# Loads in two parts and scatters of full height in the routing stage of a graph layer with experts

## The chip, the core and the metric

The kernel runs on one core of a Trainium2 chip. The time is device time in microseconds, from the first to the last instruction; the number compared is the median of several executions. The engines are PE (TensorE), DVE (VectorE), ACT (ScalarE), POOL (GpSimd) and SP (SyncE, which here only starts DMAs); sixteen DMA engines move the data.

## What is computed

6250 nodes of 256 features go through a graph attention layer with 8 heads and 200000 edges, then through a layer of 8 experts, of which each node uses the best two. Cut to what matters (`_layernorm`, `elu` and `top_k` are the usual ones):

```python
def gnn(x, src, trg):                     # x normed
    proj = (x @ Wp.T).reshape(-1, H, FO)
    s = leaky_relu(sum(proj * a_src)[src] + sum(proj * a_trg)[trg], 0.2)
    exp_s = exp(s - max(s))
    attn = exp_s / (segment_sum(exp_s, trg)[trg] + 1e-16)
    out = segment_sum(proj[src] * attn[:, :, None], trg)
    return elu(out + x @ Wskip.T + bias)
def ffn(x):                               # x normed
    top_p, top_idx = top_k(softmax(x @ Wr + br), 2)
    weights = top_p / top_p.sum()
    y = gelu((_layernorm(x) * ln_g + ln_b) @ W1 + b1) @ W2 + b2      # for each expert
    return sum(weights * y[top_idx])
x = x + gnn(_layernorm(x), src, trg)
x = x + ffn(_layernorm(x))
```

## The kernel before

It is one program of six stages, and each ends at a barrier of all engines: `edge_tables`, `node_phase` (projections, and the rows of the skip connection, which go to DRAM as `skip_rows`), `edge_phase` (gathers, softmax and sums per node; the longest), `route_phase`, `expert_phase` and `combine_phase`. Nodes are kept 125 to a tile (`NP`), 50 tiles (`NT`), since 50 x 125 is 6250; a node is a partition.

The change touches `route_phase`. It works in 10 chunks of 5 tiles (`C = 5`, `CHUNKS`), one after another, with two buffers of what is loaded and sent. For each chunk:

- SP loads the skip rows (`r_skin`, L923) and x (`r_xin`, L926), each as one DMA of 125 partitions x 5 rows of 1 KB, 640 KB. From the third chunk on it waits until VectorE has used the buffer (`skin_used`, `x_used`).
- VectorE divides the sums by the softmax denominator (L955), adds the skip rows (L960), takes the positive part plus x (L963), while ScalarE computes 1 - exp, floored at 0, for the negative part (`ex`, L1107 and L1109); L968 joins the two. Then come mean and variance, the first norm (`xl`, L989, read by PE for the logits), the choice of the two best experts (L1003 to L1021), each node's place among those of its expert (L1027 to L1035, from counts by PE), and the second norm (`r_xn`, L1042), which is what the experts get. ScalarE copies that for the second expert (L1125).
- GpSimd sends each node's row of 257 words (256 features and the row that its result goes to) into `tokens_by_expert` (in the code `xg`), an indirect DMA for each tile and each of its two experts: ten scatters of 125 rows a chunk (L1183), to the rows in `slot`.

```python
nc.gpsimd.indirect_dma_start(
    xg, bass.IndirectOffsetOnAxis(ap=slot[b][:, 2 * u + k:2 * u + k + 1], axis=0),
    xn[b][:, u, k, :], None).then_inc(sent[b], 16)
```

The order on each engine is the order written here. VectorE runs one chunk ahead with the first part: `attention(c + 1)`, `choose(c)`, `residual(c + 1)`, `places(c)`, `first_deviation(c + 1)`, `second_norm(c)`, `first_norm(c + 1)`. At the stage's end VectorE turns the counts into whole numbers (`count_ready`), on which SP starts eight DMAs of 256 rows that write `padding` behind each expert's tokens (L932) and waits for them; GpSimd waits for its last scatters.

The last stage, `combine_phase`, already loads and stores in the two parts of `NODE_PARTS`, 112 and 13 partitions (L1481).

Of the kernel before, what the change touches and what calls it, by code (L numbers as in the profile page):

```python
# [12 lines left out]
F32 = mybir.dt.float32  # L13
F32R = mybir.dt.float32r
BF16 = mybir.dt.bfloat16
I32 = mybir.dt.int32
# [68 lines left out]
def gnn_ffn(nc, x, src, dst, Wp, a_src, a_trg, Wskip, bias, Wr, br, ln_g, ln_b, W1, b1, W2, b2, out):  # L85
    table = nc.dram_tensor("proj_table", (N, ROW), F32).ap()
    skip_rows = nc.dram_tensor("skip_rows", (N, D), F32).ap()
    xg = nc.dram_tensor("tokens_by_expert", (NX * CAP, XROW), F32).ap()

    y2 = nc.dram_tensor("results_by_token", (2 * N + P, D), F32).ap()  # L90

    with ExitStack() as ctx:
        def sb(name, shape, dt=F32):
            return ctx.enter_context(nc.sbuf_tensor(name, shape, dt))

        banks = ctx.enter_context(nc.psum_tensor("banks", [P, 8, 512], F32))
        bank = [banks[:, k, :] for k in range(8)]
        m = dict(
            banks=banks,
            iota=sb("iota", [P, P]), iota_p=sb("iota_p", [P, 1]), ident=sb("ident", [P, P]),  # L100
            lower=sb("lower", [P, P]), ones=sb("ones", [P, P]), zero16=sb("zero16", [P, ROW], BF16),
            begun=ctx.enter_context(nc.semaphore("begun")),
            cap_row=sb("cap_row", [P, NX]), ident_r=sb("ident_r", [P, P], F32R),
            acc=sb("acc", [NP, NT + 2, ROW]), neg_bound=sb("neg_bound", [P, 1]),
            ln_eps=sb("ln_eps", [P, 1]), eps=sb("eps", [P, 1]),
            gaps=sb("gaps", [NP, NT]), warm=[sb(f"warm{k}", [P, 1]) for k in range(3)], weights=sb("weights", [NP, NT, 2]),
            result_row=sb("result_row", [NP, NT, 2]), counts=sb("counts", [1, NX, 4], I32),
            br=sb("br", [NP, NX]), wr=sb("wr", [P, KD, NX]),
        )
        with ExitStack() as edge_ctx:  # L110
            def esb(name, shape, dt=F32):
                return edge_ctx.enter_context(nc.sbuf_tensor(name, shape, dt))

            m.update(src_tab=esb("src_tab", [P, COLS], I32), dst_tab=esb("dst_tab", [P, COLS]),
                     place_tab=esb("place_tab", [P, (STEPS + AHEAD) * G]), key_tab=esb("key_tab", [P, (STEPS + AHEAD) * G]),
                     inside_tab=esb("inside_tab", [P, (STEPS + AHEAD) * G]),
                     base_tab=esb("base_tab", [P, STEPS + AHEAD]), tile_int=esb("tile_int", [1, 1 + STEPS + AHEAD], I32),
                     upper=esb("upper", [P, 1 + STEPS + AHEAD]), nextt=esb("nextt", [P, 1 + STEPS + AHEAD]),
                     passes=esb("passes", [1, 1], I32), st_parts=esb("st_parts", [P, NT + 2, ZC], BF16))
            edge_tables(nc, m, bank, src, dst)  # L120
            node_phase(nc, m, bank, x, Wp, a_src, a_trg, Wskip, bias, Wr, br, table, skip_rows)
            edge_phase(nc, m, bank, table)
        route_phase(nc, m, bank, x, skip_rows, xg)
        expert_phase(nc, m, bank, xg, y2, ln_g, ln_b, W1, b1, W2, b2)
        combine_phase(nc, m, y2, out)
# [742 lines left out]
def route_phase(nc, m, bank, x, skip_rows, xg):  # L868


    with ExitStack() as ctx:
        def sb(name, shape, dt=F32):
            return ctx.enter_context(nc.sbuf_tensor(name, shape, dt))
# [6 lines left out]

        C = 5
        CHUNKS = NT // C
        xin, skin = ([sb(f"{s}{b}", [NP, C, D]) for b in range(2)] for s in ("r_xin", "r_skin"))
        den = sb("den", [NP, NT, H])
        att, positive, ex = sb("att", [NP, C, D]), sb("positive", [NP, C, D]), sb("ex", [NP, C, D])
        stats, mv = sb("r_stats", [NP, C, 6]), sb("r_mv", [NP, NT, 2])
        std1, rstd1, var2, std2, rstd12 = (sb(s, [NP, NT]) for s in ("std1", "rstd1", "var2", "std2", "rstd12"))
        xl, xlt = sb("xl", [NP, C, D]), sb("xlt", [P, C * KD, NP])
        xn = [sb(f"r_xn{b}", [NP, C, 2, XROW]) for b in range(2)]
        logits, top8, pick8 = sb("logits", [NP, C, NX]), sb("top8", [NP, C, 8]), sb("pick8", [NP, C, 8], U32)  # L890
        pick, one = sb("pick", [NP, C, 2]), sb("one", [NP, C, 2, NX])
        mask = [sb(f"mask{b}", [NP, 1 + C, NX], BF16) for b in range(2)]
        lower16, ones16 = sb("lower16", [NP, NP], BF16), sb("ones16", [NP, NP], BF16)
        place, junk = sb("place", [NP, C, 2]), sb("junk", [NP, C, 2, NX])
        slot = [sb(f"slot{b}", [NP, C * 2], I32) for b in range(2)]
        padding = sb("padding", [P, FILL // P, XROW])
        crow, cwhole = sb("count_row", [1, 6, NX]), sb("count_whole", [1, NX], I32)
        wtmp = sb("wtmp", [NP, NT])
# [7 lines left out]
        xl_ready, xlt_psum, xlt_ready, logit_psum, mask_ready, ranked, slot_ready, xn_first, xn_ready = (sem(s) for s in (  # L906
            "xl_ready", "xlt_psum", "xlt_ready", "logit_psum", "mask_ready", "ranked", "slot_ready", "xn_first", "r_xn_ready"))
        dve_step, end_step, weight_exp = sem("route_step"), sem("end_step"), sem("weight_exp")
        counted, count_ready, filled = sem("counted"), sem("count_ready"), sem("filled")
        block = ctx.enter_context(nc.Block())  # L910

        def of(c):
# [2 lines left out]
        @block.sync  # L915
        def _(sp):
            def chunk(rows, c):
                return rows[c * C * NP:(c + 1) * C * NP, :].rearrange("(u p) d -> p u d", u=C)

            for c in range(CHUNKS):  # L920
                if c >= 2:
                    sp.wait_ge(skin_used, c - 1)
                sp.dma_start(skin[c % 2][:], chunk(skip_rows, c)).then_inc(skin_loaded[c % 2], 16)  # L923
                if c >= 2:
                    sp.wait_ge(x_used, c - 1)
                sp.dma_start(xin[c % 2][:], chunk(x, c)).then_inc(xin_loaded[c % 2], 16)  # L926
            sp.wait_ge(count_ready, 1)

            with sp.Fori(0, NX) as e:
                n = nc.values_load(m["counts"][0:1, bass.ds(e, 1), 0:1].rearrange("p a k -> p (a k)"),  # L930
                                   engines=[sp.engine], min_val=0, max_val=N)
                sp.dma_start(xg[bass.ds(e * CAP + n, FILL), :].rearrange("(h p) d -> p h d", p=P), padding[:]  # L932
                             ).then_inc(filled, 16)
            sp.wait_ge(filled, 16 * NX)

        @block.vector
        def _(dve):
# [12 lines left out]
            def attention(c):  # L950
                b = c % 2
                x1 = m["acc"][:, of(c), 0:D].rearrange("p u (h f) -> p u h f", h=H)
                if c:
                    dve.wait_ge(ex_ready, c)
                step(nc.vector.tensor_tensor(  # L955
                    att[:].rearrange("p u (h f) -> p u h f", h=H), x1,
                    den[:, of(c), :].unsqueeze(3).to_broadcast([NP, C, H, FO]), ALU.mult))
                settle()
                dve.wait_ge(skin_loaded[b], 16 * (c // 2 + 1))
                nc.vector.tensor_tensor(att[:], att[:], skin[b][:], ALU.add).then_inc(skin_used, 1)  # L960
                dve.wait_ge(skin_used, c + 1)
                dve.wait_ge(xin_loaded[b], 16 * (c // 2 + 1))
                nc.vector.scalar_tensor_tensor(positive[:], att[:], 0.0, xin[b][:], ALU.max, ALU.add).then_inc(x_used, 1)  # L963

            def residual(c):
# [58 lines left out]
            def places(c):  # L1024
                b = c % 2
                dve.wait_ge(ranked, c + 1)
                step(nc.vector.tensor_tensor(junk[:], one[:], rank_bank.unsqueeze(2).to_broadcast([NP, C, 2, NX]), ALU.mult))  # L1027
                with nc.allow_low_precision("whole numbers up to 50"):
                    step(nc.vector.tensor_reduce(mask[1 - b][:, 0, :], mask[b][:].rearrange("p v e -> p e v"), X, ALU.add))
                dve.wait_ge(dve_step, steps[0] - 1)  # L1030
                step(nc.vector.tensor_reduce(place[:], junk[:], X, ALU.add))
                settle()
                if c >= 2:
                    dve.wait_ge(sent[b], 16 * 2 * C * (c // 2))
                nc.vector.scalar_tensor_tensor(slot[b][:].rearrange("p (u k) -> p u k", k=2), pick[:], float(CAP), place[:],  # L1035
                                               ALU.mult, ALU.add).then_inc(slot_ready, 1)
                nc.vector.tensor_copy(xn[b][:, :, :, D], m["result_row"][:, of(c), :]).then_inc(slot_ready, 1)

            def second_norm(c):
                for u in range(C):  # L1040
                    t = c * C + u
                    nc.vector.tensor_scalar(xn[c % 2][:, u, 0, 0:D], x1_of(t), mv[:, t, 0:1], rstd12[:, t:t + 1],  # L1042
                                            ALU.subtract, ALU.mult).then_inc(xn_first, 1)

            step(nc.vector.tensor_scalar(den[:], m["acc"][:, 0:NT, D:ROW], m["eps"][0:NP, :], None, ALU.add))
# [58 lines left out]
        def _(act):  # L1104
# [17 lines left out]

            def second_copy(c):
                act.wait_ge(xn_first, C * (c + 1))
                nc.scalar.copy(xn[c % 2][:, :, 1, 0:D], xn[c % 2][:, :, 0, 0:D]).then_inc(xn_ready, 1)  # L1125

            exponential(0)
            deviations(0)
# [45 lines left out]

        @block.gpsimd
        def _(pool):
            for c in range(CHUNKS):
                b = c % 2
                pool.wait_ge(slot_ready, 2 * (c + 1))
# [354 lines left out]
```

## Time and profile before

| | us |
|---|---|
| median of 3 executions | 3241.75 (3241.1 to 3244.08) |
| span of the profiled execution | 3796.4 |
| routing stage in the profiled execution | 2835.7 to 3050.7 |

The profiled execution is a run of its own, with the profiler on, and its own time is that span: 554.65 us, 17%, longer than the median. Positions and durations below are of that execution, in microseconds from its start. A row of the timeline shows when an instruction began, how long it ran, and in brackets how long its engine had stood idle before it and what ended the wait. A row of the windows shows, for a stretch of time, how long each engine was busy, the mean busy share of the sixteen DMA engines, and what they moved.

### The profile page before, as it was taken

To read this page: it belongs to the slowest core of one execution; us is meant where nothing else is said; L and a number is where in the kernel's file an instruction comes from. 1 tells how busy PE (TensorE), PEld (TensorE's weight loads), DVE (VectorE), ACT (ScalarE), POOL (GpSimd) and SP (SyncE) were. 2 spreads that over 40 slices of the span, in tenths; PEclk is the share of its full clock that TensorE was granted. 3 is DMA by queue.
4 is the path that set the end of the run, shared out by engine and by line. 5 is a ranking of instruction groups with operands and counts; after the bars stand their busy time and mean duration, and the time that the engine had idled before them with its cause. 6 is when DMAs were issued, how large, how long until landed. Compare 5 with 4: busy or idle time off the path is not lost. (4 is left out here: it accounts for less than half of the span.)

```text
span 3796.4 us, 46157 instructions
## 1 busy us (share of the span) xinstructions
PE 2122.9 (56%) x12432; PEld 1788.7 (47%) x12433; DVE 1956.5 (52%) x5386; ACT 890.4 (23%) x2271; POOL 1821.9 (48%) x2025
## 2 busy tenths in 40 slices
PE   3755454544545554545455455444543359999990
PEld 3434343433434443434334334333433359999990
DVE  6545444444444444444444444444458746666654
ACT  1221111111111111111111111111114435555540
POOL 1026655656556656656565565655635722222110
PEclk7976767677777667677677776776765579999995
DMA  1333322323233333323333333322324442222116
GB/s 54 113 96 84 86 80 81 85 78 85 80 81 83 86 83 85 84 81 83 81 84 81 81 83 83 85 80 80 85 63 144 117 118 65 68 90 67 44 44 207
DMA packets 163652, 326.51 MB, mean 86 GB/s; under 512 B 41487, under 2 KB 95742, under 8 KB 163628
## 3 DMA queue, kind: packets, MB, share of 16 engines
q0 software_dynamic: 98560, 256.53, 24.7%
q1 hardware_dynamic: 45528, 50.33, 4.4%
q10 hardware_dynamic: 19540, 19.40, 1.6%
q8 instruction: 7, 0.11, 0.0%
q14 instruction: 17, 0.14, 0.0%
HBM read 278.03 MB, written 47.99 MB: 86 GB/s over the span
## 5 line engine op out<-in xcount | busy, mean ns | idle before, releaser
L626 POOL DMA_INDIRECT rows<-proj_table,idx x1568 | 1492.1, 952 | 1028.6 <-DVE weighed L741 612.9
L670 PE MATMUL banks<-weighed,onehot 128*128 128x264 f32 x3136 | 1147.8, 528 | 1293.5 <-DVE weighed L741 1232.4
L670 PEld LDWEIGHTS banks<-weighed,onehot 128*128 128x128 f32 x3136 | 783.1, 263 | 1475.0 <-issue 1312.5
L725 DVE TENSOR_REDUCE target<-banks 128x32 f32<-128x96 f32 x393 | 100.6, 256 | 1193.0 <-remote 1108.5
L741 DVE TENSOR_TENSOR weighed<-rows,banks 128x1024 f32<-128x1024 f32 x392 | 474.5, 1211 | 0.0
L845 ACT ACTIVATE banks<-score,neg_bound 128x32 f32<-128x32 f32 x392 | 114.1, 291 | 1387.8 <-DVE score L734 1069.5
L840 ACT CAST onehot_t<-banks 128x512 bf16<-128x512 f32 x395 | 228.2, 578 | 764.3 <-remote 740.0
L1441 POOL DMA_INDIRECT results_by_token<-yrow,goes_to x104 | 109.1, 1049 | 478.2 <-DVE yrow L1389 350.7
L707 DVE TENSOR_TENSOR onehot<-banks,key_tab 128x512 f32<-128x512 f32 x397 | 270.9, 683 | 0.0
L1328 ACT ACTIVATE hid<-banks,params 128x256 f32<-128x256 f32 x416 | 197.9, 477 | 267.5 <-PE banks L1284 261.1
L1284 PE MATMUL banks<-f_xth,w1h 128*128 128x256 f32 x832 | 236.4, 284 | 27.2 <-ACT hid L1328 14.9
L1377 DVE TENSOR_TENSOR hidl<-hid,hidh 128x256 fp32r<-128x256 f32 x416 | 169.9, 424 | 149.6 <-ACT hidh L1322 138.0
L1284 PE MATMUL banks<-f_xtl,w1h 128*128 128x256 f32 x832 | 234.4, 282 | 0.0
L1284 PE MATMUL banks<-f_xth,w1l 128*128 128x256 f32 x832 | 234.3, 282 | 0.0
L649 PEld LDWEIGHTS banks<-ident,onehot 128*128 128x128 bf16 x1584 | 150.6, 117 | 102.6 <-issue 48.2
L649 PE MATMUL banks<-ident,onehot 128*128 128x128 bf16 x1584 | 184.7, 250 | 3.8 <-DVE onehot L707 2.7
L1183 POOL DMA_INDIRECT tokens_by_expert<-r_xn,slot x100 | 130.5, 1305 | 103.8 <-issue 96.4
L1284 PEld LDWEIGHTS banks<-f_xth,w1h 128*128 128x128 f32 x832 | 158.4, 190 | 31.1 <-ACT hid L1328 16.4
L1297 PE MATMUL banks<-w2h,hidh 128*128 128x256 f32 x832 | 170.5, 286 | 0.0
L1297 PE MATMUL banks<-w2l,hidh 128*128 128x256 f32 x832 | 166.1, 281 | 0.0
L1297 PE MATMUL banks<-w2h,hidl 128*128 128x256 f32 x832 | 165.9, 281 | 0.0
L1322 ACT CAST hidh<-hid 128x256 fp32r<-128x256 f32 x416 | 161.2, 401 | 0.0
(236 smaller groups left out, 2901.1 us busy)
## 6 DMA issues: line engine op xcount, KB each, us to landing
rows<-proj_table,idx POOLq DMA_INDIRECT x1568
w_raw<-in_L_ffn_W_dram POOLq DMA_DIRECT2D x16, 1024.0 KB
xrow<-tokens_by_expert SPq DMA_DIRECT2D x106, 128.5 KB
c_y<-results_by_token SPq DMA_DIRECT2D x10, 1120.0 KB
proj_table<-trow ACTq DMA_DIRECT2D x50, 128.9 KB
xin<-in_x_dram SPq DMA_DIRECT2D x50, 125.0 KB
skip_rows<-srow ACTq DMA_DIRECT2D x50, 125.0 KB
r_skin<-skip_rows SPq DMA_DIRECT2D x10, 625.0 KB
```

Of the source, the lines that this page charges most:

```text
L626: nc.gpsimd.indirect_dma_start(rows[k][:, i, :], None, table, bass.IndirectOffsetOnAxis(ap=idx[pair][:, col:col + 1], axis=0)).then_inc(ga ...
L649: mm = nc.tensor.matmul(turn_bank[s % 2][:, i * P:(i + 1) * P], onehot16[s % ROUND][:, i, :], ident16[:], start=True, stop=True)
L670: mm = nc.tensor.matmul(acc_bank[u // 2 % 2][:, 0:ROW], onehot[u][:, i, :], weighed[:, k * SET + i, :], start=(u % 2 == 0 and i == 0), sto ...
L707: nc.vector.tensor_tensor(onehot[s % ROUND][:], node_row[s % 2].unsqueeze(1).to_broadcast(shape), m["key_tab"][:, bass.ds(ROUND * SET * it ...
L741: nc.vector.tensor_tensor(weighed[:, k * SET:(k + 1) * SET, 0:D].rearrange("p s (h f) -> p s h f", h=H), rows[k][:, :, 0:D].rearrange("p s ...
L840: nc.scalar.copy(onehot_t[s % BUF][:], turn_bank[s % 2][:]).then_inc(turn_copied[s % BUF], 1)
L1183: nc.gpsimd.indirect_dma_start(xg, bass.IndirectOffsetOnAxis(ap=slot[b][:, 2 * u + k:2 * u + k + 1], axis=0), xn[b][:, u, k, :], None).the ...
L1284: mm = nc.tensor.matmul(h_bank[j % HB][:, 0:TOK], w[:, s, k, at], v[:, k, :], start=(k == 0 and n == 0), stop=(k == KD - 1 and n == 2))
L1297: mm = nc.tensor.matmul(y_bank[h][:, 0:D], v[:, j, h * P:(h + 1) * P], w[:, s, j, :], start=(j == 0 and n == 0), stop=(j == JH - 1 and n = ...
L1322: nc.scalar.copy(hidh[:, j, :], hid[:, j, :]).then_inc(hid_high, 1)
L1328: nc.scalar.activation(hid[:, j, :], h_bank[j % HB][:, 0:TOK], ACT.Gelu, bias=params[:, s, B1 + j:B1 + j + 1]).then_inc(h_ready[j % HB], 1)
L1377: nc.vector.tensor_tensor(hidl[:, j, :], hid[:, j, :], hidh[:, j, :].bitcast(F32), ALU.subtract).then_inc(hid_low, 1)
```

## The change

Each of the twenty loads becomes two, of partitions 0 to 111 and 112 to 124, and VectorE waits for both. `r_xn` and `slot` get 128 partitions. GpSimd fills them at the start of the stage: `slot` with numbers of spare rows behind the experts' rows (of which `tokens_by_expert` gets 128 more), `r_xn` from partition 96 on with zeros; VectorE later writes the first 125 partitions of both as before. The scatters then send all 128 partitions. VectorE waits for the filling (`cleared`) ahead of its first L963.

```diff
-    xg = nc.dram_tensor("tokens_by_expert", (NX * CAP, XROW), F32).ap()
+    xg = nc.dram_tensor("tokens_by_expert", (NX * CAP + P, XROW), F32).ap()
...
+        SPARE = NP // 32 * 32
...
-        xn = [sb(f"r_xn{b}", [NP, C, 2, XROW]) for b in range(2)]
+        xn = [sb(f"r_xn{b}", [P, C, 2, XROW]) for b in range(2)]
...
-        slot = [sb(f"slot{b}", [NP, C * 2], I32) for b in range(2)]
+        slot = [sb(f"slot{b}", [P, C * 2], I32) for b in range(2)]
...
-                sp.dma_start(skin[c % 2][:], chunk(skip_rows, c)).then_inc(skin_loaded[c % 2], 16)
+                for part in NODE_PARTS:
+                    sp.dma_start(skin[c % 2][part], chunk(skip_rows, c)[part]).then_inc(skin_loaded[c % 2], 16)
...
-                sp.dma_start(xin[c % 2][:], chunk(x, c)).then_inc(xin_loaded[c % 2], 16)
+                for part in NODE_PARTS:
+                    sp.dma_start(xin[c % 2][part], chunk(x, c)[part]).then_inc(xin_loaded[c % 2], 16)
...
-                dve.wait_ge(skin_loaded[b], 16 * (c // 2 + 1))
+                dve.wait_ge(skin_loaded[b], 16 * len(NODE_PARTS) * (c // 2 + 1))
...
+                if c == 0:
+                    dve.wait_ge(cleared, 4)
...
-                dve.wait_ge(xin_loaded[b], 16 * (c // 2 + 1))
+                dve.wait_ge(xin_loaded[b], 16 * len(NODE_PARTS) * (c // 2 + 1))
...
         @block.gpsimd
         def _(pool):
+            for b in range(2):
+                nc.gpsimd.iota(slot[b][:], [[1, 2 * C]], base=NX * CAP + (2 * b - NP * 4) * C,
+                               channel_multiplier=4 * C).then_inc(cleared, 1)
+                pool.wait_ge(cleared, 2 * b + 1)
+                nc.gpsimd.memset(xn[b][SPARE:P], 0.0).then_inc(cleared, 1)
+                pool.wait_ge(cleared, 2 * b + 2)
```

The other lines of the diff write `[0:NP]` where VectorE and ScalarE write `slot` and `r_xn`.

SP's queue at the start of the routing stage, before (a row is an instruction; the names are tile and tensor, and what it waits for stands in brackets):

```order
L915 UNCONDITIONAL_BRANCH [waits barrier_Pool_Activation_PE_DVE_SP_release]
L923 DMA r_skin<-skip_rows 125x5x256
L926 DMA r_xin<-in_x_dram 125x5x256
L923 DMA r_skin<-skip_rows 125x5x256
L926 DMA r_xin<-in_x_dram 125x5x256
L923 DMA r_skin<-skip_rows 125x5x256 [waits skin_used]
```

and of the change:

```order
L916 UNCONDITIONAL_BRANCH [waits barrier_Pool_Activation_PE_DVE_SP_release]
L925 DMA r_skin<-skip_rows 112x5x256
L925 DMA r_skin<-skip_rows 13x5x256
L929 DMA r_xin<-in_x_dram 112x5x256
L929 DMA r_xin<-in_x_dram 13x5x256
L925 DMA r_skin<-skip_rows 112x5x256
L925 DMA r_skin<-skip_rows 13x5x256
L929 DMA r_xin<-in_x_dram 112x5x256
L929 DMA r_xin<-in_x_dram 13x5x256
L925 DMA r_skin<-skip_rows 112x5x256 [waits skin_used]
```

Eight DMAs in place of four lie ahead of the first wait, and the x of the first chunk stands third and fourth. GpSimd's queue at the same place, of the change (before, the branch was followed at once by the first scatter):

```order
L1180 UNCONDITIONAL_BRANCH [waits barrier_Pool_Activation_PE_DVE_SP_gather]
L1183 IOTA slot 128x10
L1186 MEMSET r_xn 32x2570 [waits cleared]
L1183 IOTA slot 128x10 [waits cleared]
L1186 MEMSET r_xn 32x2570 [waits cleared]
L1194 DMA tokens_by_expert<-r_xn,slot 53376x257 [waits r_xn_ready,slot_ready,cleared]
```

Four instructions stand ahead of the scatters, each behind the one before it. VectorE's order is the same; of the change, from the stage's start (L963 of before is L968 here):

```order
L1050 TENSOR_SCALAR den<-acc,eps 125x400
L1052 RECIPROCAL den<-den 125x400 [waits route_step]
L958 TENSOR_TENSOR att<-acc,den 125x1280 [waits route_step]
L963 TENSOR_TENSOR att<-att,r_skin 125x1280 [waits skin_loaded0,route_step]
L968 SCALAR_TENSOR_TENSOR positive<-att,r_xin 125x1280 [waits xin_loaded0,skin_used,cleared]
```

The last of these rows has one more thing to wait for, `cleared`.

## Rows read from the trace of the kernel before

**Rows 1.** The page, first line.

```profile
span 3796.4 us, 46157 instructions
```

**Rows 2.** Timeline, start of the routing stage; columns: start us, us, engine, line, operation [idle before].

```profile
2835.75 0.28 SPq L923 DMA_DIRECT2D r_skin<-skip_rows  x1
...
2835.79 0.43 DVE L1045 TENSOR_SCALAR den<-acc,eps 125x400 f32<-125x400 f32 x1 [0.32 <-PEq L549]
2836.46 1.77 SPq L926 DMA_DIRECT2D r_xin<-in_x_dram  x1
...
2838.94 1.49 DVE L955 TENSOR_TENSOR att<-acc,den 125x1280 f32<-125x1280 f32 x1
...
2844.66 1.49 DVE L960 TENSOR_TENSOR att<-att,r_skin 125x1280 f32<-125x1280 f32 x1 [4.23 <-DMA r_skin<-skip_rows]
...
2847.49 1.36 ACT L1109 ACTIVATE ex<-ex,ones 125x1280 f32<-125x1280 f32 x1
...
2850.40 1.49 DVE L963 SCALAR_TENSOR_TENSOR positive<-att,r_xin 125x1280 f32<-125x1280 f32 x1 [4.25 <-DMA r_xin<-in_x_dram]
...
2852.70 1.48 DVE L968 TENSOR_TENSOR acc<-positive,ex 125x1280 f32<-125x1280 f32 x1
```

**Rows 3.** Windows: stretch, us, busy of PE, PEld, DVE, ACT, POOL, PEclk, DMA share, GB/s.

```profile
2840.00:2850.00 10.00, 0.00 (x0) 0.00 (x0) 1.92 (x2) 3.76 (x3) 0.00 (x0) 0.50 0.34 110
...
3043.00:3047.00 4.00, 0.00 (x0) 0.00 (x0) 0.00 (x0) 0.00 (x0) 0.08 (x1) 0.50 0.83 211
...
3057.00:3059.00 2.00, 0.00 (x0) 0.00 (x0) 0.00 (x0) 0.00 (x0) 0.00 (x0) 0.50 1.06 359
3728.00:3732.00 4.00, 0.00 (x0) 0.00 (x0) 2.48 (x7) 0.00 (x0) 0.00 (x0) 0.50 1.01 257
```

**Rows 4.** Timeline, middle of the routing stage, VectorE and GpSimd.

```profile
2865.86 0.20 DVE L1003 TENSOR_TENSOR logits<-banks,br 125x40 f32<-125x40 f32 x1 [1.99 <-PE banks L1152]
...
2874.16 1.70 DVE L989 TENSOR_SCALAR xl<-acc,r_mv,rstd 125x256 f32<-125x256 f32 x5
...
2882.66 0.20 DVE L1003 TENSOR_TENSOR logits<-banks,br 125x40 f32<-125x40 f32 x1 [1.93 <-PE banks L1152]
...
2899.84 0.20 DVE L1003 TENSOR_TENSOR logits<-banks,br 125x40 f32<-125x40 f32 x1 [1.74 <-PE banks L1152]
...
2908.31 1.89 DVE L989 TENSOR_SCALAR xl<-acc,r_mv,rstd 125x256 f32<-125x256 f32 x5
...
2910.59 2.49 POOL L1183 DMA_INDIRECT tokens_by_expert<-r_xn,slot  x1 [1.77 <-ACT r_xn L1125]
```

**Rows 5.** By line: duration ns min/median/max, first and last start; the last row is L1441's.

```profile
L1183 POOL DMA_INDIRECT tokens_by_expert<-r_xn,slot x100: 1175/1187/2493, 2876.6 to 3041.9; - x100
L626 POOL DMA_INDIRECT rows<-proj_table,idx x1568: 943/949/1146, 247.8 to 2807.8; - x196
L1441 POOL DMA_INDIRECT results_by_token<-yrow,goes_to x104: 972/993/1382, 3096.7 to 3713.7; - x104
DMA to landing us min/median/max: 2.4/2.4/3.9
```

**Rows 6.** Waits in the routing stage, GpSimd: us in total, times, longest.

```profile
POOL tokens_by_expert L1183 <- ACT r_xn L1125: 7.4, 5, 1.8
```

**Rows 7.** Timeline, end of the routing stage, GpSimd and SP.

```profile
3029.85 15.26 SPq L932 DMA_DIRECT2D tokens_by_expert<-padding  x8
...
3041.90 1.18 POOL L1183 DMA_INDIRECT tokens_by_expert<-r_xn,slot  x1 [0.30 <-issue]
```

**Rows 8.** Waits of SP's queue in the routing stage: us in total, times, longest.

```profile
SPq L923 <- DVE att L960: 73.1, 7, 14.9
...
SPq L871 <- DMA tokens_by_expert<-padding: 4.5, 1, 4.5
```

**Rows 9.** Timeline, start of the program: a long GpSimd memset and VectorE beside it.

```profile
1.95 11.53 POOL L180 MEMSET acc<- 125x13728 f32 x1
...
2.35 11.21 DVE L213 TENSOR_SCALAR ident<-iota,iota_p 128x128 f32<-128x128 f32 x1
```

More of the change, by code:

```diff
@@ L908, in route_phase @@
         dve_step, end_step, weight_exp = sem("route_step"), sem("end_step"), sem("weight_exp")
-        counted, count_ready, filled = sem("counted"), sem("count_ready"), sem("filled")
+        counted, count_ready, filled, cleared = sem("counted"), sem("count_ready"), sem("filled"), sem("cleared")
         block = ctx.enter_context(nc.Block())
@@ L1034, in places @@
                     dve.wait_ge(sent[b], 16 * 2 * C * (c // 2))
-                nc.vector.scalar_tensor_tensor(slot[b][:].rearrange("p (u k) -> p u k", k=2), pick[:], float(CAP), place[:],
+                nc.vector.scalar_tensor_tensor(slot[b][0:NP].rearrange("p (u k) -> p u k", k=2), pick[:], float(CAP), place[:],
                                                ALU.mult, ALU.add).then_inc(slot_ready, 1)
-                nc.vector.tensor_copy(xn[b][:, :, :, D], m["result_row"][:, of(c), :]).then_inc(slot_ready, 1)
+                nc.vector.tensor_copy(xn[b][0:NP, :, :, D], m["result_row"][:, of(c), :]).then_inc(slot_ready, 1)
             def second_norm(c):
@@ L1041, in second_norm @@
                     t = c * C + u
-                    nc.vector.tensor_scalar(xn[c % 2][:, u, 0, 0:D], x1_of(t), mv[:, t, 0:1], rstd12[:, t:t + 1],
+                    nc.vector.tensor_scalar(xn[c % 2][0:NP, u, 0, 0:D], x1_of(t), mv[:, t, 0:1], rstd12[:, t:t + 1],
                                             ALU.subtract, ALU.mult).then_inc(xn_first, 1)
@@ L1124, in second_copy @@
                 act.wait_ge(xn_first, C * (c + 1))
-                nc.scalar.copy(xn[c % 2][:, :, 1, 0:D], xn[c % 2][:, :, 0, 0:D]).then_inc(xn_ready, 1)
+                nc.scalar.copy(xn[c % 2][0:NP, :, 1, 0:D], xn[c % 2][0:NP, :, 0, 0:D]).then_inc(xn_ready, 1)
             exponential(0)
```

## The prediction

> **What bounds the kernel now.** I began with the page: a span of 3796.4 us under the profiler [rows 1]. The median of the runs without it is 3241.75 us, 555 us less, and no view says where these 555 us lie. So the terms below are absolute microseconds of the routing stage (2835.7 to 3050.7 of the span, some 6% of it), and I subtract them from the median; if everything there shrank by 3241.75/3796.4 the sum would shrink by a seventh, which I keep for the range. The chain that ended last names only the combine stage's loads, so the rest is read from the timeline.
>
> *Start of the stage* [rows 2]. SP issues the first skip load at 2835.75 and the first x load at 2836.46. VectorE has its own work done at 2840.43 (den, reciprocal, first product) and then stands idle twice: 4.23 us until the skip rows are in, 4.25 us until x is in. Nothing else runs. The loads move at 110 GB/s with the 16 DMA engines busy 0.34 on average [rows 3], which is what five busy engines of sixteen would show (0.31). One load is 640 KB, 5.7 us at that rate. The first wait ends 8.9 us after the first issue, so 3.2 us of it are fixed (start and completion).
>
> *Middle.* From chunk to chunk VectorE's step L1003 comes at 2865.86, 2882.66, 2899.84: periods of 16.80 and 17.18 us [rows 4]. No load is waited for any more. VectorE is the pace; it waits 1.7 to 2.0 us a chunk for the logits, on a chain that runs through its own norms. GpSimd is nearly as long: ten scatters of 1.19 + 0.30 us, two of them stretched by about 1 us each (one took 2.49), are some 17 us; it waits for ScalarE's copy only five times, 7.4 us in all [rows 4 to 6].
>
> *End.* The last scatter is issued at 3041.90 and takes 1.18. SP issues the eight padding DMAs from 3029.85 to 3045.11 [rows 7] and then waits 4.5 us for them, until 3049.6 [rows 8]. A scatter lands 2.4 us after its issue in the expert stage [rows 5], so GpSimd would be through at about 3045.5. The padding ends this stage, and SP's pitch (15.26 us for eight) sets most of it.
>
> **Part 1: loads of 112 and 13 partitions.** The same bytes in two DMAs. If 112 partitions use 16 engines at the same rate for each engine as now, the rate is 110/5 × 16 = 352 GB/s: 1.8 us for a 640 KB pair. Two rows bound it: the expert weights, loaded in rows of 1 KB on all engines, run at 359 GB/s; the combine stage, whose loads have this very 112/13 split, begins at 257 GB/s with the engines all busy (1.01) [rows 3], which gives 2.5 us.
> The Trainium skill says the same of the engines (DMA: Bandwidth & Descriptors, "Why a DMA increments its semaphore by 16 and not by 1"): a DMA uses the largest number up to 16 that divides its outermost sizes, 5 for 125, 16 for 112, 13 for 13. By that rule, the share of 0.34 agrees.
> Working: at 352 GB/s the skip rows are in at 2835.75 + 3.2 + 1.8 = 2840.75, x at 2842.55. Then L960 starts at 2840.75. ScalarE's ex is ready 4.19 us after L960 starts (in the rows L960 at 2844.66, L1109 over at 2848.85), so at 2844.95; L968 starts 2.30 us after L963 (2850.40 to 2852.70), so at 2844.85. The later one counts: 2845.0 instead of 2852.70, a gain of **7.7 us**. At 257 GB/s: skip 2841.5, x 2844.0, L968 at 2846.3, gain **6.4**. I take **7.4**, nearer the first, since it is these same tensors whose rate per engine is known. VectorE's wait of 8.5 us doesn't go whole: what is late next is ScalarE's ex.
> SP's extra issues cost nothing: the unblocked ones are some 0.7 us apart, four are 2.8 us, and x's second half is issued at about 2837.9, 3.2 us before 2841.1, earlier than its data anyway. In the middle SP waits 73.1 us on VectorE [rows 8], so twenty more issues hide there.
>
> **Part 2: iota and memset on GpSimd, and VectorE's wait for them before L963.** The memset is 2570 elements per partition. The one row of a large GpSimd memset is 13728 elements in 11.53 us [rows 9], 0.84 ns each, so 2.2 us, twice, plus two iotas of about 0.15 us and three handovers of some 0.2: done about 5.3 us after 2835.7, at 2841.0. L963 is due at 2842.5. The cover is 1.5 us, so no cost; without cover (memsets at twice the time) it would be 3 us. Queued behind the wait on VectorE are L963 and everything after it. But rows 9 also show a VectorE TENSOR_SCALAR that took 11.21 us beside that memset, and L1045 is such an operation. Here the iota and a semaphore lie ahead of the memset, L1045 goes at 2835.79 and lasts 0.43. I charge **0.2 us** (behind the iota); the other end is one memset, 2.2 us, of which 0.3 is covered by the skip rows: 1.9.
>
> **Part 3: scatters of 128 rows.** For GpSimd's time the rows give two answers. By rows: 1.187 × 128/125 = 1.22 us. By form: the 128-row scatter of the expert stage takes 0.993 (median), the 128-row gather 0.949 [rows 5], against 1.187 for 125 rows, though it has 3 rows more. I take 0.99: same direction, nearly the same row length. GpSimd then needs some 2 us less per chunk. Since VectorE is the pace, little of it counts. What does count is that L989 takes 1.70 us before the scatters begin and 1.89 beside them [rows 4], and that the period was 16.80 once and then 17.18. The full difference over nine chunks would be 3.4 us; I take a third where GpSimd now has idle time just before the next copy is ready, **1.0 us**. With 1.22 us a scatter, GpSimd would need 0.3 more a chunk against a slack of about 0.17: 1.2 us lost. Range -1.2 to 3.4.
> At the end ten shorter scatters finish 2 us or more earlier, but the padding bounds there. The engines are busy 0.83 at 211 GB/s from 3043 to 3047, after the last scatter's issue [rows 3]: padding is queued behind scatters. Alone, a 256-row DMA should land about 2.9 us after its issue (2.4 of the 128-row scatter, and 0.5 for the other half at that rate): 3048.0 in place of 3049.6. Range 0 to 1.6, taken **1.0**. The spare rows add 3 × 1028 B each, 0.3 MB in all, 1 us spread over the stage, hidden.
>
> **Sum:** 7.4 - 0.2 + 1.0 + 1.0 = 9.2 us, 3241.75 - 9.2 = **3232.6 us**. All bounds on the good side give 7.7 + 3.4 + 1.6 = 12.7 (3229.0); on the bad side 6.4 - 1.9 - 1.2 + 0 = 3.3 (3238.5). The stages after it start earlier and are otherwise the same.
>
> **Rivals.**
> *A, the memset holds VectorE.* L1045 waits out a memset, as in rows 9, or the clearing ends after L963 is due. The gain falls by 1.9 to 3: 9.2 - 1.9 = 7.3, 3234.4; at worst 3235.6. For it: the 11.21 us. Against: the iota and the handover come first.
> The Trainium skill has this as a rule (SBUF — State Buffer, "Who interferes with whom"): a VectorE operation in a two-port mode, which TENSOR_SCALAR can be, and a GpSimd instruction exclude each other, and the one that issues first keeps the port for its whole length. By that rule the order of starts decides; rows 9 agree.
> *B, the loads are no faster.* 1 KB rows may be limited by something other than the number of engines, or the stage's fixed latencies grow with four DMAs; then only the 2 us of part 3 stay: 3239.8. Against: 359 GB/s at the same row length.
> *C, slower: GpSimd becomes the pace.* Its ten scatters are within 0.2 us of VectorE's period. If one takes x us more, nine chunks lose 9 × (10x - 0.17). Against the 7.2 us of the start that breaks even at x = 0.1; at x = 0.3 (1.49 us a scatter) it is 25 us, 3241.75 - 7.2 + 25.5 = 3260. For it: descriptors for all engines instead of some could cost GpSimd more. Against: both 128-row forms are shorter than the 125-row form.
> *D, the split is made but the stall isn't on the unprofiled path as long,* everything a seventh smaller: 8 us, 3233.9.
>
> **Chances.** Forecast, with D in it, 0.68; A 0.12; B 0.12; C 0.05; 0.03 for what I don't see. A measurement of this kernel tells 0.2% (6.5 us) from no change. Faster by over that: 0.65 of the forecast, 0.08 of A, 0.02: 0.75. Within: 0.03 + 0.04 of A + 0.12 of B: 0.19. Slower: C and 0.01: 0.06. The range 3228 to 3239 holds the forecast's bounds and A; it leaves out B and C.
>
> **What would show it.** In the trace of the changed kernel: VectorE's idle time before L960 and L963 under 1 us each in place of 4.2; DMA share near 1 in the first 4 us of data; L968 of chunk 0 some 9.5 us after L1045, not 16.9; L1045 at 0.43 us (several us means A); two memsets of about 2.2 us; scatters of about 0.99 us and a wait for ScalarE's copy in every chunk (none, and a period above 17.2, means C); SP's wait for the padding near 3 us in place of 4.5. Wrong outright: a stall of the same length at the start, or a loss in a later stage.

## The result: 6 us faster, with a loss at the stage's end that the sum did not hold

| | kernel before | changed kernel |
|---|---|---|
| median of 20 runs each, us | 3243.31 | 3237.18 |
| range of the runs, us | 3241.10 to 3248.68 | 3234.75 to 3240.23 |
| span of the trace, us | 3238.8 | 3235.1 |

The ratio is 0.9981, with a 95% interval of 0.9974 to 0.9987: 6.1 us less, where 9.2 were forecast. The time lies in the forecast range (3228 to 3239). It is 0.4 us short of the 0.2% (6.5 us) that the prediction set as the least that can be told from no change: by its own bins the outcome is "within", which it gave 0.19, and not the faster one with 0.75. The interval lies wholly on the faster side of 1.

The kernel before was traced again, beside the experiments (run e1_base below); its span there was 3238.8 us, near its time, and not 3796.4 as in [rows 1]. The routing stage was as long in both traces, 213.9 and 214.8 us. The 555 us lay ahead of the stage (`den` came at 2835.79 in the first trace, and at 2278.11 in the second), the stage's microseconds were true ones, and nothing had to be scaled down. "Before" is this second trace from here on.

The stage begins with VectorE's `den` (L1045, now L1050) and ends when all engines have passed the barrier that closes it (L871; the first instruction behind it is ScalarE's table load, 0.1 us later). Other lines moved as well: L960, L963, L968 are now L963, L968, L973; L1003 is L1008; L1183 is L1194.

**The start.** Timeline of the changed kernel: start, us, engine, line, operation, with the idle time before it in brackets.

```profile
2282.75 1.10 SPq L925 DMA_DIRECT2D r_skin<-skip_rows  x2
2282.79 0.43 DVE L1050 TENSOR_SCALAR den<-acc,eps 125x400 f32<-125x400 f32 x1 [0.32 <-PEq L549]
2282.98 2.42 POOL L1186 MEMSET r_xn<- 32x2570 f32 x1
2283.91 0.85 SPq L929 DMA_DIRECT2D r_xin<-in_x_dram  x2
...
2285.67 2.24 POOL L1186 MEMSET r_xn<- 32x2570 f32 x1
...
2288.49 1.49 DVE L963 TENSOR_TENSOR att<-att,r_skin 125x1280 f32<-125x1280 f32 x1 [1.05 <-DMA r_skin<-skip_rows]
...
2291.42 1.49 DVE L968 SCALAR_TENSOR_TENSOR positive<-att,r_xin 125x1280 f32<-125x1280 f32 x1 [1.45 <-DMA r_xin<-in_x_dram]
...
2293.73 1.48 DVE L973 TENSOR_TENSOR acc<-positive,ex 125x1280 f32<-125x1280 f32 x1
```

The same place of the kernel before, second trace:

```profile
2278.11 0.43 DVE L1045 TENSOR_SCALAR den<-acc,eps 125x400 f32<-125x400 f32 x1 [0.32 <-PEq L549]
...
2286.59 1.49 DVE L960 TENSOR_TENSOR att<-att,r_skin 125x1280 f32<-125x1280 f32 x1 [3.85 <-DMA r_skin<-skip_rows]
...
2292.33 1.49 DVE L963 SCALAR_TENSOR_TENSOR positive<-att,r_xin 125x1280 f32<-125x1280 f32 x1 [4.25 <-DMA r_xin<-in_x_dram]
...
2294.62 1.48 DVE L968 TENSOR_TENSOR acc<-positive,ex 125x1280 f32<-125x1280 f32 x1
```

The two waits of [rows 2] are now 1.05 and 1.45 us. The residual (L973, once L968: it joins the two parts) starts 10.94 us after `den` in place of 16.51: 5.6 us gained. Against the first trace, where it was 16.91, it would be 6.0. `den` waited 0.32 us in both kernels, so the clearing held it up by nothing, and the clearing is over at 2287.91, 3.5 us before L968 wants it.

Windows of the changed kernel: stretch, us, busy time of PE, PEld, DVE, ACT, POOL, then PEclk, DMA share, GB/s.

```profile
2285.00:2286.00 1.00, 0.00 (x0) 0.00 (x0) 0.97 (x2) 0.00 (x0) 0.87 (x3) 0.50 1.10 353
2286.00:2289.00 3.00, 0.00 (x0) 0.00 (x0) 1.95 (x2) 0.00 (x0) 1.90 (x1) 0.50 1.13 243
2289.00:2293.00 4.00, 0.00 (x0) 0.00 (x0) 2.50 (x3) 2.94 (x3) 0.00 (x0) 0.50 1.13 227
```

All sixteen engines are busy, against a third of them in [rows 3]. But the rate is 353 GB/s for one microsecond only, and then 243 and 227, below both of the prediction's rates (352 and 257).

**The middle.** The logits step of chunks 1 and 2, the changed kernel:

```profile
2323.68 0.20 DVE L1008 TENSOR_TENSOR logits<-banks,br 125x40 f32<-125x40 f32 x1 [1.93 <-PE banks L1157]
...
2340.47 0.20 DVE L1008 TENSOR_TENSOR logits<-banks,br 125x40 f32<-125x40 f32 x1 [1.93 <-PE banks L1157]
```

The period, from one chunk's logits step to the next, is 16.8 us here and in all later chunks. In the second trace of before the first period was 16.80 too, as in [rows 4], and the eight later ones 17.15 to 17.22. The groups by line and shape (busy us, mean ns), with the scatters (ns min/median/max) and GpSimd's wait for ScalarE's copy (us, times, longest), say where it comes from. The changed kernel:

```profile
L994 DVE TENSOR_SCALAR xl<-acc,r_mv,rstd 125x256 f32<-125x256 f32 x50 | 17.0, 406 | 0.0
L1047 DVE TENSOR_SCALAR r_xn<-acc,r_mv,rstd 125x256 f32<-125x256 f32 x50 | 17.0, 407 | 0.0
...
L1194 POOL DMA_INDIRECT tokens_by_expert<-r_xn,slot x100: 957/963/2197, 2317.5 to 2476.9; - x100
...
POOL tokens_by_expert L1194 <- ACT r_xn L1130: 48.8, 10, 29.6
```

The kernel before:

```profile
L989 DVE TENSOR_SCALAR xl<-acc,r_mv,rstd 125x256 f32<-125x256 f32 x50 | 19.3, 449 | 0.0
L1042 DVE TENSOR_SCALAR r_xn<-acc,r_mv,rstd 125x256 f32<-125x256 f32 x50 | 18.5, 434 | 0.0
```

A scatter of 128 rows costs GpSimd 0.963 us, of 125 rows 1.184. VectorE's two norms, which run beside them, fall from 449 and 434 ns to 406 and 407 on average. But an average hides what happened. By minimum, median and longest of the fifty first norms (ns), before and then changed:

```profile
L989 DVE TENSOR_SCALAR xl<-acc,r_mv,rstd x50: 394/402/615, 2299.2 to 2454.6; 125x256 f32<-125x256 f32 x50
```

```profile
L994 DVE TENSOR_SCALAR xl<-acc,r_mv,rstd x50: 401/405/414, 2298.3 to 2450.8; 125x256 f32<-125x256 f32 x50
```

The median hardly moved. In the kernel before, 21 of the hundred norms took 571 to 615 ns, and the other 79 about 402. Each of the 21 began 0.67 to 0.74 us after a scatter's start and ended 0.09 to 0.10 us after that scatter's end, as this norm did (timelines of GpSimd and of VectorE, the kernel before):

```profile
2349.54 1.18 POOL L1183 DMA_INDIRECT tokens_by_expert<-r_xn,slot  x1 [0.30 <-issue]
...
2350.21 0.60 DVE L989 TENSOR_SCALAR xl<-acc,r_mv,rstd 125x256 f32<-125x256 f32 x1
```

None of the 79 was running when a scatter ended. In the changed kernel no norm takes over 431 ns, although 17 of them were running when a scatter ended. Run e9 below shows both in one trace: with ten scatters of 125 rows among the 128-row ones it has three norms of 575 to 605 ns, all beside those ten, and one period of 17.16 us at that place, the others 16.8. So the longer period comes with norms that stretch to the end of a 125-row scatter by 0.19 us; two such norms on the way from chunk to chunk would make up the 0.37 (an estimate). Why a 128-row scatter doesn't hold them no run shows. GpSimd now waits for the copy in all ten chunks, so VectorE alone sets the pace.

**The end.** Timeline of the end of the stage, GpSimd, SP and ScalarE, and the waits of SP's queue in the stage (us, times, longest). The changed kernel:

```profile
2467.21 13.51 SPq L935 DMA_DIRECT2D tokens_by_expert<-padding  x8
...
2476.94 0.96 POOL L1194 DMA_INDIRECT tokens_by_expert<-r_xn,slot  x1 [0.30 <-issue]
...
2489.83 1.28 ACT L1356 ACT_TABLE_LOAD   x1 [23.49 <-PEq L871]
...
SPq L871 <- PEq L871: 6.5, 1, 6.5
SPq L871 <- DMA tokens_by_expert<-padding: 2.2, 1, 2.2
```

The kernel before:

```profile
2471.63 14.15 SPq L932 DMA_DIRECT2D tokens_by_expert<-padding  x8
...
2483.66 1.17 POOL L1183 DMA_INDIRECT tokens_by_expert<-r_xn,slot  x1 [0.31 <-issue]
...
2492.07 1.28 ACT L1345 ACT_TABLE_LOAD   x1 [21.42 <-PEq L871]
...
SPq L871 <- DMA tokens_by_expert<-padding: 5.2, 1, 5.2
SPq L871 <- PEq L871: 0.6, 1, 0.6
```

SP's wait for the padding fell from 5.2 to 2.2 us, better than forecast. Yet from the padding's first issue to the table load it takes 22.6 us, and took 20.4. A new wait stands behind it: SP is at the barrier 6.5 us early. The line names TensorE's queue as the one that let it go, but TensorE was at the barrier long before (its own DRAIN there came at 2461.9). Of the queues' own instructions at L871, which no busy time counts, one stands out (ns min/median/max, first and last start). GpSimd in the changed kernel, and in the kernel before:

```profile
L871 POOLq DRAIN  x1: 8227/8227/8227, 2481.4 to 2481.4; - x1
```

```profile
L871 POOLq DRAIN  x1: 876/876/876, 2490.9 to 2490.9; - x1
```

GpSimd has waited until its scatters have landed when it comes to this DRAIN, the last thing ahead of the barrier. It now takes 8.2 us in place of 0.9. Before, it ended 0.5 us after SP was through; now it ends 6.3 us after. The barrier is passed some 0.16 us after the later of the two, in these traces and in all that follow. In these 7 us next to no data moves (changed kernel):

```profile
2482.00:2489.00 7.00, 0.00 (x0) 0.00 (x0) 0.00 (x0) 0.00 (x0) 0.00 (x0) 0.50 0.01 2
```

**Accounts of the stage** (before 213.9 us, changed 207.0): start -5.6; middle -3.5 (the padding's first issue comes 184.4 us after `den`, and came at 193.5: 9.1 in all); the end up to SP's leave -3.7; the DRAIN +5.9. Sum -6.9. The medians differ by 6.1. The spans of the two traces differ by only 3.7, since the stages ahead, which the change doesn't touch, took 4.7 us more in the changed kernel's trace, and those behind 1.5 less.

### The profile page after: what moved, and what is told of

The parts are those of the page before. It is cut to its first block and busy times, and to the rows that moved or that the text cites. A ratio compares the mean times of both kernels' runs of the same rounds, so it can differ in the third digit from the quotient of the medians.

```text
span 3235.1 us, 46181 instructions
## 1 busy us (share of the span) xinstructions
PE 2104.3 (65%) x12432; PEld 1767.5 (55%) x12433; DVE 1935.0 (60%) x5386; ACT 861.4 (27%) x2271; POOL 1808.8 (56%) x2029
## 5 line engine op out<-in xcount | busy, mean ns | idle before, releaser
L670 PE MATMUL banks<-weighed,onehot 128*128 128x264 f32 x3136 | 1115.8, 517 | 761.9 <-DVE weighed L741 761.9
L670 PEld LDWEIGHTS banks<-weighed,onehot 128*128 128x128 f32 x3136 | 756.7, 253 | 945.0 <-issue 789.3
L731 DVE TENSOR_TENSOR raw_score<-rows,target 128x32 f32<-128x32 f32 x392 | 75.3, 192 | 768.8 <-DMA rows<-proj_table,idx 768.8
L614 POOL COPY idx<-src_tab 128x8 int32 x196 | 39.8, 203 | 233.0 <-issue 232.3
```

Source lines behind the costliest of these rows:

```text
L670: mm = nc.tensor.matmul(acc_bank[u // 2 % 2][:, 0:ROW], onehot[u][:, i, :], weighed[:, k * SET + i, :], start=(u % 2 == 0 and i == 0), sto ...
```

## The experiments

The theory after the result: the loads give some 5.6 us, the scatters of 128 rows some 7 us of pace and landing, and of these the DRAIN takes back 5.9. Rivals for the DRAIN: the clearing (iota and memset) causes it; the last scatter or the last burst does; it is work left over from the scatters, and would pass while others wait; the number of such scatters in the whole stage decides. All runs are in one table; "residual" (its start), "padding" (its first issue) and "barrier" (when the stage ends) are us after `den`, "SP through" and "DRAIN starts" us after the padding's first issue.

| run | residual | padding | SP through | DRAIN starts / takes | barrier | median, us (runs) | ratio to before, 95% |
|---|---|---|---|---|---|---|---|
| e1_base | 16.5 | 193.5 | 19.8 | 19.3 / 0.88 | 213.9 | 3240.4 (1) | |
| changed kernel | 10.9 | 184.4 | 16.1 | 14.2 / 8.23 | 207.0 | 3237.2 (20) | 0.9981, 0.9974 to 0.9987 |
| e2_loads_only | 10.8 | 187.8 | 19.7 | 19.3 / 0.88 | 208.2 | 3233.7 (11) | 0.9981, 0.9972 to 0.9990 |
| e3_scatters_only | 16.3 | 189.7 | 15.9 | 12.8 / 8.23 | 210.9 | 3238.5 (11) | 0.9997, 0.9988 to 1.0006 |
| e4_last_chunk_125 | 10.7 | 184.2 | 19.8 | 19.0 / 0.88 | 204.2 | 3231.9 (9) | 0.9977, 0.9967 to 0.9986 |
| e5_last_one_125 | 10.9 | 184.5 | 16.6 | 14.1 / 8.23 | 207.0 | 3236.5 (1) | |
| e6_last_one_128 | 10.4 | 183.9 | 19.2 | 18.5 / 0.88 | 203.4 | 3232.3 (1) | |
| e7_last_five_125 | 10.8 | 184.3 | 18.6 | 18.1 / 8.23 | 210.9 | 3238.5 (1) | |
| e8_pair_first | 10.2 | 183.8 | 15.8 | 12.8 / 8.23 | 205.0 | 3231.5 (1) | |
| e9_chunk0_125 | 10.5 | 184.4 | 16.3 | 13.9 / 0.88 | 200.9 | 3229.3 (5) | 0.9960, 0.9946 to 0.9975 |
| e10_chunk8_125 | 10.5 | 184.9 | 17.2 | 15.4 / 0.88 | 202.3 | 3229.6 (1) | |
| e11_ten_more | 10.8 | 186.4 | 16.1 | 13.7 / 6.60 | 206.8 | 3234.1 (1) | |
| e12_best | 10.5 | 184.4 | 16.2 | 13.9 / 0.88 | 200.7 | 3232.1 (5) | 0.9959, 0.9945 to 0.9972 |

Runs with a ratio were timed against the kernel before on the same chip. Medians of different chips don't compare (before had 3239.9 beside e1 to e4, 3241.8 beside e9, 3245.5 beside e12); the stage in the trace does.

### e1_base

The kernel before, unchanged.

> The kernel before once more, for a second trace of it. In the first the edge phase was some 550 us longer than in the timed runs, in the changed kernel's trace it was not. Expected: a span near 3242 us, and the routing stage as in the first trace: L968 16.9 us after L1045, a period of 17.18 us from chunk to chunk, GpSimd's scatters at 1.19 us, the padding's issue 194.1 us after L1045, and the barrier that ends the stage 20.8 us after that. If the first trace was disturbed in the routing stage too, these numbers move, and the difference to the changed kernel with them.

It gave the second trace that stands above: the residual 16.5 us after `den`, a period of 17.16, scatters of 1.18 us, the padding's issue at 193.5 and the barrier 20.4 us behind it, each within 0.6 us of what was expected.

### e2_loads_only and e3_scatters_only: each part alone

e2 has the loads in two pieces and the rest as before; e3 has whole loads, and all else of the change:

```diff
-                for part in NODE_PARTS:
-                    sp.dma_start(skin[c % 2][part], chunk(skip_rows, c)[part]).then_inc(skin_loaded[c % 2], 16)
+                sp.dma_start(skin[c % 2][:], chunk(skip_rows, c)).then_inc(skin_loaded[c % 2], 16)
```

(x likewise, and VectorE waits for 16 instead of 32.)

> Only the loads are changed (112 and 13 partitions), the scatters stay at 125 rows, and nothing is filled. Both theories of the end of the stage (see the run with the last chunk at 125 rows) expect the same here: L968 of chunk 0 comes 10.9 us after L1045 instead of 16.9, the period stays at 17.18, the end of the stage stays at 20.8 us after the padding's issue with a short last instruction of GpSimd (0.9 us). Sum: 6.0 us less than before, about 3237.3.

> Only the scatters are changed (128 rows, with iota and memset on GpSimd), the loads stay at 125 partitions. Expected: the start as before (L968 16.9 us after L1045), a period of 16.8 us (3.4 us less over nine chunks), the padding through 4 us earlier, and GpSimd's last instruction before the barrier at 8 us, which gives 5.9 of it back: 1.6 us less than before, about 3241.7. If the long last instruction needed the new loads too, it would be short here and the gain 7.5 us: 3235.8.

e2 gains 5.7 us in the stage (6.0 expected), all of it at the start, and e3 3.0 (1.6 expected): together 8.7, against 6.9 for both (1.3 of the 1.8 between them is that the DRAIN starts 12.8 us after the padding's first issue in e3, and 14.2 in the changed kernel). By the timed runs the loads alone can't be told from the whole change (both ratios 0.9981, with intervals of some 0.1% to either side), and the scatters alone can't be told from no change (0.9997). The scatters alone move the end of the stage by only 3.0 us, although SP is through 7.6 us earlier: the long DRAIN is theirs, with or without the new loads.

### e4, e5, e6, e7: scatters of 125 rows in the last chunk

All four are the changed kernel with

```diff
+                        rows = NP if c == CHUNKS - 1 else P
-                            xg, bass.IndirectOffsetOnAxis(ap=slot[b][:, 2 * u + k:2 * u + k + 1], axis=0),
-                            xn[b][:, u, k, :], None).then_inc(sent[b], 16)
+                            xg, bass.IndirectOffsetOnAxis(ap=slot[b][0:rows, 2 * u + k:2 * u + k + 1], axis=0),
+                            xn[b][0:rows, u, k, :], None).then_inc(sent[b], 16)
```

e4 so for the whole last chunk; e5 for its last scatter alone (`and 2 * u + k == 9`), e6 for all of it but the last (`< 9`), e7 for its last five (`>= 5`).

> The changed kernel, but the ten scatters of the last chunk send 125 rows. Theory 1: the 8 us of GpSimd's last instruction (DRAIN) are work left over from a burst of 128-row scatters, so they shrink to under 1 us here; the padding is as slow as before, the barrier comes 20.8 us after the padding's issue: 9.6 us less than before, about 3233.7. Theory 2: they come from the iota and memset on GpSimd in this stage, whatever is scattered last; they stay near 8 us: about 3237 to 3238.

> The changed kernel with only the very last of the hundred scatters at 125 rows. How long is GpSimd's DRAIN before the barrier? It was 8.23 us behind ten scatters of 128 rows and 0.88 us behind ten of 125. If its length goes with the number of 128-row scatters in the last burst: 7.5 us (nine tenths of the difference). If the last scatter alone decides it: 0.9 us.

> The reverse: nine scatters of 125 rows in the last chunk, then one of 128. By the number of 128-row scatters in the burst: 1.6 us. If the last scatter alone decides: 8.2 us.

> Five scatters of 128 rows, then five of 125 in the last chunk. By the number of 128-row scatters in the burst: 4.6 us. If work is left over from them and done meanwhile: less, since the five last take 7.4 us: near 0.9. If the last alone decides: 0.9.

The clearing is in all four, and in e4 and e6 the DRAIN is short: it isn't the cause. Nor is the last scatter: of 125 rows in e5 with a long DRAIN, of 128 in e6 with a short one. e7 answers two more. Its DRAIN starts 18.1 us after the padding's first issue, 4 us later than in the changed kernel, and takes the same 8.23. So it isn't a remainder that passes with time. None of the three lengths in between that were forecast by the number of 128-row scatters in the last burst came (7.5, 1.6 and 4.6 us): it is the whole 8.23 or 0.88. GpSimd's DRAIN in e5, e6 and e7:

```profile
L871 POOLq DRAIN  x1: 8232/8232/8232, 2481.0 to 2481.0; - x1
```

```profile
L871 POOLq DRAIN  x1: 882/882/882, 2483.1 to 2483.1; - x1
```

```profile
L871 POOLq DRAIN  x1: 8232/8232/8232, 2482.6 to 2482.6; - x1
```

e4 came out by theory 1: the stage is 9.7 us shorter than before's (9.6 expected), and its median 7.9 us under before's on the same chip. What theory 1 says of the reason, work left over from a burst, falls with e7. The price of e4 is the landing: SP is through only at 19.8 us, as before.

### e8_pair_first: no loads behind the first pair

At the start SP issues chunk 1's loads right behind chunk 0's. Here it waits:

```diff
+                if c == 1:
+                    sp.wait_ge(x_used, 1)
```

> The changed kernel, but SP starts the loads of the second chunk only when VectorE has used the first chunk's x. In the changed kernel L963 starts 5.7 us after the den instruction and L968 8.6 us; the forecast had 5.0 and 6.8. If the loads queued behind the first pair slow it, they are gone here: 5.0 and 6.8 to 7.3. If sixteen engines get no more than some 220 GB/s from these tensors by themselves, nothing moves: 5.6 and 8.5. The total is of no interest.

The residual starts at 10.2 us, against 10.4 to 10.9 in the nine traces with the new loads and without this wait; in e12, which has it too, at 10.5. L963 and L968 of the changed kernel start 5.4 and 7.9 us after `den` here, between the two forecasts; without the wait they come at 5.4 to 5.7 and 8.1 to 8.6, and in e12 at 5.9 and 8.2. Loads queued behind the first pair thus cost 0.7 us at most, and perhaps nothing. That isn't the 1.8 us by which the start missed its 7.4.

### e9_chunk0_125 and e10_chunk8_125: ten scatters of 125 rows elsewhere

The edit of e4 with `c == 0`, and with `c == CHUNKS - 2`.

> The changed kernel with the ten scatters of the first chunk at 125 rows, all later ones at 128. GpSimd's DRAIN was 8.23 us with 100, 99 or 95 scatters of 128 rows in the stage (the shorter ones last) and 0.88 us with 91, 90 or none. If the count over the whole stage decides it, it is 0.88 us here, the barrier comes 16.5 us after the padding's issue, and the time is some 13 us below before: 3227. If the last burst decides it (ten of 128): 8.23 us, the time of the changed kernel or a few tenths more: 3234 to 3237.

> The same with the last chunk but one. By the count over the stage: 0.88 us. By the last ten scatters: 8.23 us. If a longer window than the last chunk counts (the last 16 to 20, of which ten are 128 here), it could be either, and then differs from the run with the first chunk at 125 rows.

In e9 the last ninety scatters, and so all that GpSimd does in the 150 us ahead of the DRAIN, are as in the changed kernel; only the first ten differ. Its DRAIN is short:

```profile
L871 POOLq DRAIN  x1: 882/882/882, 2477.7 to 2477.7; - x1
```

The stage takes 200.9 us, 6.1 less than the changed kernel's, and the median is 12.4 us under before's on the same chip (some 13 expected). In e10 ten scatters of 125 rows in the ninth chunk give the same 0.88. So the length of the DRAIN hangs on what was sent in total, not on when in the stage.

### e11_ten_more: is it the count of 128-row scatters?

e9, with ten more scatters of 128 rows in chunk 1 into a tensor of their own that nothing reads.

```diff
+                        if c == 1:
+                            nc.gpsimd.indirect_dma_start(
+                                extra_rows, bass.IndirectOffsetOnAxis(ap=slot[b][:, 2 * u + k:2 * u + k + 1], axis=0),
+                                xn[b][:, u, k, :], None).then_inc(extra, 16)
```

> The kernel with the first chunk at 125 rows (90 scatters of 128 rows in the stage, DRAIN 0.88 us), and in the second chunk ten more scatters of 128 rows, of the same rows into a tensor of its own that nothing reads: 100 of 128 rows and ten of 125. If the number of 128-row scatters since the stage began decides the length of the DRAIN (91 short, 95 long), it is 8.23 us again. If what matters is that the first ones are of 125 rows, 0.88. The barrier comes 16.5 us after the padding's issue where it is short, some 22 where it is long.

The DRAIN is long again, but 6.60 us, not 8.23:

```profile
L872 POOLq DRAIN  x1: 6598/6598/6598, 2480.0 to 2480.0; - x1
```

So ten more scatters bring most of it back; neither of the two lengths expected came, and the count of 128-row scatters alone isn't the rule. In all: 95, 99 or 100 of 128 rows with 5, 1 or 0 of 125 give 8.23; 90 or 91 with 10 or 9 give 0.88; none with 100 gives 0.88; 100 with 10 give 6.60.

### e12_best

e8's wait and e9's rows together.

> The kernel with the first chunk at 125 rows, and SP starts the second chunk's loads only when VectorE has used the first chunk's x. Expected: DRAIN 0.88 us, L963 5.4 and L968 8.0 us after the den instruction (in the runs without that wait 5.4 to 5.7 and 8.2 to 8.6), and a time at or some 0.3 us below that of the run with the first chunk at 125 rows: 0.996 of before.

The DRAIN is 0.88 us. L963 came at 5.9 and L968 at 8.2, both later than expected, and the stage is 200.7 us, e9's within 0.2; the wait adds nothing to be seen. Both are 0.4% under the kernel before (0.9960 and 0.9959), about twice the change's gain, and e9 has fewer edits. They have the shortest stages of those tried; but as long as nobody knows what sets the DRAIN, e9's ten scatters are a number that was found, and another size of the problem may want another.

## Why the prediction was right, and where its sum was not

- **Which 555 us.** Right: the stage was as long as in the first trace, and rival D's scaling falls.
- **Start, 7.4 forecast, 5.6 measured (5.7 in e2): mis-sized.** The step from "these tensors' rate per engine is known" to 352 GB/s failed. One engine gave 22 GB/s when five worked (110 by 5), and 14 to 15 when sixteen did (227 and 243 by 16). The 257 of the combine stage, taken as the lower bound, was nearer: it gave x at 8.2 us after `den` and L968 of before at 10.5, and they came at 8.6 and 10.9 here, and at 8.1 to 8.6 and 10.4 to 10.9 in the other traces with these loads. So two of the prediction's signs failed: waits under 1 us each (1.05 and 1.45), and the residual at 9.5. Of the 1.8 missing microseconds 0.4 are the second trace of before, which starts faster than the first (16.5 against 16.9), and e8 puts at most 0.7 down to queued loads. What limits the sixteen together was not tested. The Trainium skill's rule on the number of engines (DMA: Bandwidth & Descriptors, "Why a DMA increments its semaphore by 16 and not by 1") held, share 1.13 for 0.34. Another line of that page ("Rules for kernel authors") says of two transfers to disjoint partition halves not to bother, because both halves already use all sixteen engines. By it e2 would have gained nothing, and it gained 5.7 us: here the whole transfer kept only a third of the engines busy (0.34).
- **Clearing, 0.2 forecast, nothing measured: right.** Memsets of 2.42 and 2.24 us (2.2), done 5.2 us after the first issue (5.3), `den` at 0.43 us and not later than before. Rival A falls.
- **Middle, 1.0 forecast, 3.5 measured: mis-sized.** The scatter's 0.96 us (0.99) was right. "I take a third" was wrong: all of the 0.37 us went in each of the eight longer periods, 2.9 us together, since it had been VectorE's norms held to the end of a scatter, not idle time of GpSimd. Another 0.6 went between the last logits step and the padding. The prediction had the row that shows one such norm (1.89 for 1.70 us) and the 3.4, and discounted them; the 3.4 itself counted nine periods, of which the first, 16.80 in its own rows, had nothing to lose. That it lies so near the measured 3.5 is chance. Rival C falls; GpSimd waits 48.8 us in all for the copy.
- **End, 1.0 forecast, 3.7 gained and 5.9 lost: a term missing.** The padding's wait fell to 2.2 us (about 3). What failed is the step that had GpSimd through at 3045.5 and "the padding ends this stage". The 2.4 us of landing came from the expert stage, where no padding shares the engines; in the second trace the median landing beside the padding is 5.0. The DRAIN behind the landing of the last scatter starts at 3049.6 in that same trace, 7.7 us after the last scatter's issue, and ended 0.5 us after SP was through: GpSimd and not the padding ended the stage even then. That DRAIN counts as no busy time and was in no term; that trace had a row to warn of it, the 3.57 us of GpSimd's DRAIN behind the expert stage's 104 scatters of 128 rows, but none that told of 8.2.
- **Rival B** (the loads are no faster) falls with e2. The sum came to 6.9 in the traces since 2.5 us too little in the middle and 2.7 too little at SP's end stood against 1.6 too much at the start (its 0.2 for the clearing in it) and the 5.9.

The case of a faster kernel was right for the reason given, the loads: e2 has the gain, and e3 has none that the timed runs can tell. That the gain came within 3.1 us of the forecast is partly luck: errors of 5.2 us one way and 7.5 the other.

## What to carry to other kernels

Look at every queue's last instruction ahead of a barrier, those that count as no busy time too: a wait that ends on an idle engine's queue is a sign that another queue had one. When a change makes the last-arriving engine faster, price the next one's whole way to the barrier. And let a change of two parts be tried apart: here one part alone could not be told from both, and both with the first ten scatters left at 125 rows were worth twice as much. An average that moves a little can be a few instances that moved a lot: ask for minimum, median and longest.

## What the runs showed of the hardware

- GpSimd's DRAIN after a series of scatters takes 0.88, 6.60 or 8.23 us by what was sent before, and 3.57 in the expert stage. The scatters have landed by then, and the engines are busy 0.01 while it lasts. Which count of rows, descriptors or transfers decides is open, and whether it starts with the stage or counts the 1568 gathers ahead of it too; by rows sent in the stage, 12500, 12770 and 12773 give 0.88, 12785, 12797 and 12800 give 8.23, and 14050 give 6.60, so it doesn't simply grow.
- Scatters of 128 rows are cheaper for GpSimd (0.96 against 1.18 us), and with them both the scatters and the padding beside them land sooner. From issue to landing at the stage's end, median us, first of the changed kernel, then of the kernel before, with the padding that goes out at the same time:

```profile
tokens_by_expert<-padding SPq DMA_DIRECT2D x8, 257.0 KB, 3.6
...
tokens_by_expert<-r_xn,slot POOLq DMA_INDIRECT x10, 3.8
```

```profile
tokens_by_expert<-padding SPq DMA_DIRECT2D x8, 257.0 KB, 4.5
...
tokens_by_expert<-r_xn,slot POOLq DMA_INDIRECT x13, 5.0
```

- A VectorE TENSOR_SCALAR of 125x256 that began 0.67 to 0.74 us after the start of a 125-row scatter lasted until 0.09 to 0.10 us after that scatter's end, 571 to 615 ns in place of 402: 21 of a hundred in the kernel before, 3 in e9 and none in the changed kernel. They are the 3.8 us by which the two norms' busy time fell, about what the middle gained (3.5).
